# A Mamba block with a routed MLP on one core: the first norm's root and the scaling of duT move to GpSimd instructions of another form

## What is computed

```python
h = _layernorm(x) * (1 + ca) + sa
x = x + ga * _L0_attn_ref(h, ...)      # gate, conv of 4 taps, sigmoid, selective scan over 16 states, product Wo
h = _layernorm(x) * (1 + cb) + sb
x = x + gb * _L0_ffn_ref(h, ...)       # router, 8 experts of 352, top 2
```

## Time and profile before

| | |
|---|---|
| three runs | 697.56, 698.61, 700.04 us |
| the profiled execution | 697.62 us, span 695.80 us |
| busy, share of the span | PE 88%, DVE 79%, ACT 77%, POOL 74%, weight loads 74% |
| mean granted TensorE clock | 0.984 |
| head, to the first scan | 58.2 us |
| steps, first to last scan | 58 to about 513 us |
| the experts' tiles and the combination | to 695.8 us |

### The profile page before, as it was taken

One profiled execution on the slowest core, in us unless ns is written; L12 is line 12 of the kernel. 1 busy time (PEld: TensorE's weight loads), 2 busy tenths in 40 slices (PEclk: granted clock), 3 DMA queues, 4 the chain that ended last, 5 costly groups with the idle time before them and its releaser, 6 DMA issues.

```text
span 695.8 us, 14462 instructions
## 1 busy us (share of the span) xinstructions
PE 615.6 (88%) x4435; PEld 512.3 (74%) x4435; DVE 552.0 (79%) x1170; ACT 535.4 (77%) x1000; POOL 517.3 (74%) x453
## 2 busy tenths in 40 slices
PE   3986889989988998997999898769789999999995
PEld 3444757867767675785777677658578999999994
DVE  4347779999989999999999999989986586555554
ACT  3268998997998997999799799797834756566650
POOL 3147969988799899989989999986964647644441
PEclk9999999999999999999999999899999999999998
DMA  7030336434943454534455335466711223222545
GB/s 237 0 123 2 102 86 161 135 93 129 320 122 106 115 129 128 162 101 109 119 148 136 105 100 129 128 182 178 177 30 55 65 62 86 81 69 65 152 145 193
DMA packets 65194, 82.92 MB, mean 119 GB/s; under 512 B 6960, under 2 KB 55152, under 8 KB 61024
## 3 DMA queue, kind: packets, MB, share of 16 engines
q1 hardware_dynamic: 59648, 70.78, 37.2%
q0 software_dynamic: 4320, 9.12, 4.0%
q10 hardware_dynamic: 1152, 2.10, 0.8%
HBM read 52.19 MB, written 29.78 MB: 118 GB/s over the span
## 4 chain that ended last, share of the span: by engine, by line
PE 43%; ACT 36%; DVE 11%; issue 7%; DMA 1%; POOL 1%; DVEq 0%; SPq 0%; ACTq 0%; POOLq 0%
PE psum L589 26%; PE psum L593 16%; ACT S L1006 12%; ACT dA L1014 11%; DVE ring L1370 5%; ACT L953 1%; ACT xn L918 1%; ACT soft L946 1%; ACT soft L945 1%; ACT soft L953 1%; ACT soft L950 1%; ACT L1014 1%; DMA ring<-results 1%; ACT hT L900 1%; ACT psum L958 1%
## 5 line engine op out<-in xcount | busy, mean ns | idle before, releaser
L559 POOL TENSOR_TENSOR ring<-ring,Cb 128x1024 f32<-128x1024 f32 x128 | 279.6, 2186 | 36.7 <-DVE ring L1370 36.2
L593 PEld LDWEIGHTS psum<-ident,S 128*128 128x128 f32 x1024 | 118.6, 143 | 113.5 <-issue 67.7
L593 PE MATMUL psum<-ident,S 128*128 128x128 f32 x1024 | 159.2, 279 | 42.7 <-DVE ring L1370 14.3
L1014 ACT ACTIVATE dA<-delta,A 128x512 f32<-128x512 f32 x256 | 178.6, 716 | 10.3 <-DVE ring L1370 10.1
L1006 ACT ACTIVATE S<-duT,BT 128x256 f32<-128x256 f32 x384 | 166.4, 501 | 24.3 <-DVE duT L1110 20.2
L593 PE MATMUL psum<-ident,ring 128*128 128x128 f32 x1088 | 159.5, 278 | 4.2 <-DMA ring<-results 3.8
L1370 DVE TENSOR_TENSOR_SCAN ring<-dA,state,psum 128x512 f32<-128x512 f32 x128 | 157.6, 1265 | 1.0 <-PE psum L593 0.4
L1370 DVE TENSOR_TENSOR_SCAN ring<-dA,psum 128x512 f32<-128x512 f32 x128 | 150.2, 1206 | 8.8 <-PE psum L593 8.2
L593 PEld LDWEIGHTS psum<-ident,ring 128*128 128x128 f32 x1088 | 129.5, 144 | 5.2 <-DMA ring<-results 4.3
L581 POOL DMA_INDIRECT results<-xn,result_at x71 | 68.7, 968 | 74.6 <-DVE xn L1503 64.9
L589 PE MATMUL psum<-uT,S 128*128 128x128 f32 x852 | 107.2, 275 | 1.0 <-DVE uT L1481 1.0
(11 more groups left out here) (218 smaller groups left out, 734.2 us busy)
## 6 DMA issues: line engine op xcount, KB each, us to landing
Cb<-c_rows SPq DMA_DIRECT2D x32, 1024.0 KB, 6.0
token_rows<-zeros SPq DMA_DIRECT2D x64, 272.0 KB, 7.1
uT<-token_rows SPq DMA_DIRECT2D x71, 68.0 KB, 1.8
ring<-results SPq DMA_DIRECT2D x8, 512.0 KB, 5.0
xT<-in_xT SPq DMA_DIRECT2D x4, 512.0 KB, 4.9
out_T<-xT ACTq DMA_DIRECT2D x8, 256.0 KB, 2.8
stage<-in_xT SPq DMA_DIRECT2D x6, 256.0 KB, 7.7
gateup_w<-in_gate SPq DMA_DIRECT2D x1, 1408.0 KB, 9.5
```

Source lines behind the costliest of these rows:

```text
L559: nc.gpsimd.tensor_tensor(ring[:, k % RING, :, 0:BANK], ring[:, k % RING, :, 1:], Cb[:, group_ % 2, own, :].unsqueeze(1).to_broadcast([P, ...
L593: return nc.tensor.matmul(out, block_in, ident[at, at], is_transpose=True, start=start, stop=True, skip_group_check=True)
L1014: nc.scalar.activation(dA[:, (k * HALVES + a) % DA_SLOTS, :], delta[:, s % 2, a, :], ACT.Exp, scale=A[:, a, n:n + 1]).then_inc(da_ready, 1)
```

## The change

It has four parts.

1. The root of segments 0 and 1 is taken in the same way as that of the others: DVE adds eps, POOL takes the power, DVE multiplies. ACT's Ln and Exp and four of DVE's five instructions go. The new steps stand right behind the statistics of segment 1, in `front_roots(0, FIRST)`.
2. The root of segments 2 to 7 is shared in the same way: DVE adds eps and later multiplies by minus mean in one instruction, POOL takes the power alone. DVE's two instructions stand right behind its last statistics, in `front_roots(FIRST, CHUNKS)`; POOL's stays in gap 19.
3. For the second norm DVE adds eps, in gap 18.
4. POOL's `scale_in` issues one tensor_scalar for each chunk, with the column of BT as a scalar of each partition and a second operation (times 1.0), in place of one tensor_tensor with a broadcast column. `add_bias` gets a second operation as well (times 1.0, where there was none).

```diff
 def pool_scaled(k):
-    return sum(pool_chunks(j) > 0 for j in range(k + 1))
+    return sum(pool_chunks(j) for j in range(k + 1))
...
-            def root(v, shifted, out, steps, count, done):
-
-                nc.gpsimd.tensor_scalar(shifted, v, LN_EPS, 1.0, ALU.add, ALU.mult).then_inc(steps, 1)
-                pool.wait_ge(steps, count)
-                nc.gpsimd.tensor_tensor(out, shifted, minus_half[:, 0:shifted.shape[1]], ALU.pow).then_inc(done, 1)
+            def front_root(first, last, shifts):
+
+                pool.wait_ge(fshift_ready, shifts)
+                nc.gpsimd.tensor_tensor(frs[:, 0, first:last], frs[:, 0, first:last], minus_half[:, first:last], ALU.pow
+                                        ).then_inc(froot_ready, 1)
...
             def tail_root(f):
-                pool.wait_ge(tstat_ready, CS * (f + 1))
-                root(tstat[:, :, 1], trs[:, 0, :], trs[:, 1, :], tstep, f + 1, trs_ready)
+                pool.wait_ge(tshift_ready, f + 1)
+                nc.gpsimd.tensor_tensor(trs[:, :], trs[:, :], minus_half[:, 0:CS], ALU.pow).then_inc(trs_ready, 1)
...
             def add_bias(b):
                 pool.wait_ge(stat_filled, SEG * (b + 1))
-                nc.gpsimd.tensor_scalar(xT[:, b * SEQ:(b + 1) * SEQ], xT[:, b * SEQ:(b + 1) * SEQ], gabo[:, b:b + 1], None,
-                                        ALU.add).then_inc(gabo_added, 1)
+                nc.gpsimd.tensor_scalar(xT[:, b * SEQ:(b + 1) * SEQ], xT[:, b * SEQ:(b + 1) * SEQ], gabo[:, b:b + 1], 1.0,
+                                        ALU.add, ALU.mult).then_inc(gabo_added, 1)
...
                 if window == -1 and gap == 19:
-                    pool.wait_ge(fstat_ready, CHUNKS)
...
+                    front_root(FIRST, CHUNKS, 2)
...
-                    nc.gpsimd.tensor_tensor(S[:, k % S_SLOTS, CS - own:, :], duT[:, s % 2, CS - own:, :],
-                                            BT[:, s % 2, CS - own:, n:n + 1].to_broadcast([P, own, MLP]), ALU.mult
-                                            ).then_inc(scaled_pool, 1)
-
+                    for c in range(CS - own, CS):
+                        nc.gpsimd.tensor_scalar(S[:, k % S_SLOTS, c, :], duT[:, s % 2, c, :], BT[:, s % 2, c, n:n + 1], 1.0,
+                                                ALU.mult, ALU.mult).then_inc(scaled_pool, 1)
+
+            front_root(0, FIRST, 1)
             pool.wait_ge(mod_step, MOD_STEPS)
...
+                if gap == 18:
+                    dve.wait_ge(tstat_ready, CS * (f + 1))
+                    V.tensor_scalar(trs[:, :], tstat[:, :, 1], LN_EPS, None, ALU.add).then_inc(tshift_ready, 1)
...
+            def front_roots(first, last):
+
+                part = slice(first, last)
+                dve.wait_ge(fstat_ready, last)
+                V.tensor_scalar(frs[:, 0, part], fstat[:, part, 1], LN_EPS, None, ALU.add).then_inc(fshift_ready, 1)
+                dve.wait_ge(froot_ready, int(first > 0) + 1)
+                V.scalar_tensor_tensor(frs[:, 1, part], fstat[:, part, 0], -1.0, frs[:, 0, part], ALU.mult, ALU.mult
+                                       ).then_inc(frs_ready, 1)
+
             for f in range(SEG):
                 raw_stats(f)
+            front_roots(0, FIRST)
...
                     if (window, gap) == (-1, 10):
                         for f in range(SEG + 3, SEGS):
                             raw_stats(f)
+                        front_roots(FIRST, CHUNKS)
```

More of the change, by code:

```diff
@@ L93, in adaln_kernel @@
         xT = sb("xT", [P, NTOK])
+        minus_half = sb("minus_half", [P, NTOK // P])
         ident = sb("ident", [P, P])
@@ L99, in adaln_kernel @@
         zeros = sb("zeros", [P, ROW])
-        eps = sb("eps", [P, 1])
-        minus_half = sb("minus_half", [P, NTOK // P])
         w1c = sb("w1c", [P, CONVK, MLP])
@@ L145, in adaln_kernel @@
         fstat = sb("fstat", [P, CHUNKS, 2])
-        frs = sb("frs", [P, 5, CHUNKS])
+        frs = sb("frs", [P, 2, CHUNKS])
         tbn = sb("tbn", [P, CS, 6])
         tstat = sb("tstat", [P, CS, 2])
-        trs = sb("trs", [P, 2, CS])
+        trs = sb("trs", [P, CS])
         u = sb("u", [P, 2, HALVES, BANK])
@@ L262, in adaln_kernel @@
                              "dbias_filled"))
-        flog, fseed, tstep, trs_ready = (sem(n) for n in ("flog", "fseed", "tstep", "trs_ready"))
-        fstep, frs_ready = ([sem(f"{n}{k}") for k in range(2)] for n in ("fstep", "frs_ready"))
+        trs_ready, froot_ready, frs_ready, fshift_ready, tshift_ready = (
+            sem(n) for n in ("trs_ready", "froot_ready", "frs_ready", "fshift_ready", "tshift_ready"))
         staged = [sem(f"staged{k}") for k in range(2)]
@@ L292, in adaln_kernel @@
         GROUP_STEPS = tuple(steps[-1] for steps in TABLE_STEPS)
-        MOD_STEPS = 26
+        MOD_STEPS = 25
         CONSTS = 9
@@ L912, in front @@
                         act.wait_ge(filled["raw"], f - SEG + 1)
-                    act.wait_ge(frs_ready[int(f >= SEG)], 1)
+                    act.wait_ge(frs_ready, min(f // SEG, 1) + 1)
                     wait(act, filled["xn"], f)
@@ L918, in front @@
                         nc.scalar.activation(xn[0][:, c * P:(c + 1) * P], source[:, c * P:(c + 1) * P], ACT.Identity,
-                                             scale=frs[:, 3, at], bias=frs[:, 4, at]).then_inc(read["raw"], 1)
+                                             scale=frs[:, 0, at], bias=frs[:, 1, at]).then_inc(read["raw"], 1)
                 if gap in (22, 28):
@@ L969, in tail @@
                                    ).then_inc(read["rows"], 1)
[L971 to L979, removed]
             def routing(gap, f):
@@ L1018, in _ @@
             nc.scalar.activation(siluc[:, :], cT[:, :], ACT.Silu).then_inc(siluc_ready, 1)
-            act.wait_ge(mod_step, 2)
-            for step in range(2):
-                front_seeds(step)
             act.wait_ge(loaded["attn"], 16 * ATTN_LOADS)
@@ L1373, in _ @@
             V.memset(mean_w[:, :], 1.0 / HID).then_inc(mod_step, 1)
-            V.memset(eps[:, :], LN_EPS).then_inc(mod_step, 1)
             V.memset(both[:, :], 0.0).then_inc(mod_step, 1)
@@ L1388, in _ @@
             V.tensor_copy(mod[:, :, :], bank(4)[:, 0:6 * BATCH].rearrange("p (k b) -> p k b", k=6)).then_inc(mod_step, 1)
-            dve.wait_ge(mod_step, 14)
+            dve.wait_ge(mod_step, 13)
             gates = mod[:, 2:6:3, :]
             V.tensor_scalar(modt[:, :, :], gates, -1.0, 0.25, ALU.mult, ALU.max).then_inc(mod_step, 1)
-            dve.wait_ge(mod_step, 15)
+            dve.wait_ge(mod_step, 14)
             V.tensor_tensor(modt[:, :, :], modt[:, :, :], gates, ALU.max).then_inc(mod_step, 1)
             V.tensor_scalar(mod[:, 1:5:3, :], mod[:, 1:5:3, :], 1.0, None, ALU.add).then_inc(mod_step, 1)
+            dve.wait_ge(mod_step, 16)
+            V.tensor_scalar(gates, gates, 0.0, 2.0, ALU.is_ge, ALU.mult).then_inc(mod_step, 1)
             dve.wait_ge(mod_step, 17)
-            V.tensor_scalar(gates, gates, 0.0, 2.0, ALU.is_ge, ALU.mult).then_inc(mod_step, 1)
+            V.scalar_tensor_tensor(gates, gates, -1.0, modt[:, :, :], ALU.add, ALU.mult).then_inc(mod_step, 1)
             dve.wait_ge(mod_step, 18)
-            V.scalar_tensor_tensor(gates, gates, -1.0, modt[:, :, :], ALU.add, ALU.mult).then_inc(mod_step, 1)
-            dve.wait_ge(mod_step, 19)
             V.tensor_scalar(gabo[:, :], mod[:, 2, :], bo[:, 0:1], None, ALU.mult).then_inc(mod_step, 1)
@@ L1425, in _ @@
             V.reduce_sum(zhalf[:, :], conv[:, :, :], AX.X).then_inc(const_ready, 1)
[L1427 to L1438, removed]
             V.tensor_tensor(w1c[:, :, :], w1.unsqueeze(1).to_broadcast([P, CONVK, MLP]),
```

7 lines of the change are left out of this document (1 added, 6 removed).

## The result

The change is slower: 707.48 us median of four runs (706.66 to 708.59) against 698.51 of four runs of the kernel before, ratio 1.0132, 95% interval 1.0112 to 1.0151, or 9.0 us. The profiled execution has a span of 704.9 us. The forecast was 701.7, with a range from 694.5 to 706.5: the direction was right, the size was not, and the measured time lies outside the range. Differences between experiments are therefore good to 1 or 2 us, and the ratios to the kernel before are the safer numbers.

What follows compares the result with a forecast made beforehand. The prediction took the chain over PE and ACT as the bound, with POOL busy 74% but 1% of the chain; -0.8 + 4.4 + 0.8 - 1.0 - 0.3 = +3.1 us gave 701.7, range 694.5 to 706.5.

Steps and rivals of the forecast that it cites:

- Small things: Second norm's eps goes from POOL to DVE's idle time at gap 18; with a memset and constants' placement, -0.3 us.
- rival of the prediction: PE's waits for S fully recovered, 697.5 (0.20); POOL pacing the steps, 694.7 (0.17); slower POOL additions and S, 714 (0.13).
- signs of being wrong: POOL's S above 0.6 us; first scan before 61; segments shorter by over 1 us each; first root's power over 2 us.
- the one on segments 2 to 5: Sign of being right in the steps: segments 2 to 5 each shorter by under 0.5 us.
- First root: Head, segments 0 and 1: DVE and POOL replace ACT's root; xn's transposes start at 16.7, not 17.50, -0.8 us.
- Second root: Head, segments 2 to 7: DVE waits for POOL's power of 24 columns ahead of softplus, +4.4 us.
- the clock: Head: PE's clock drops while it waits over 5 us for delta, slowing two groups of transposes, +0.8 us.
- POOL's S: Steps: each 256-column piece takes 0.40 us in the new form, so PE waits less, -1.0 us over the steps.
- the slow form's case: POOL's scaling and bias addition cost 2.58 ns a column after all: +16 us, 714, chance 0.13.
- POOL would now be done well before: Segment 4: POOL's S would end well before PE needs it, but DVE limits the gain to about 0.4 us.
- the four waits of PE: One wait for POOL's S in each of segments 2 to 5; recovered whole, they would bring 4 x 1.3 = 5.2 us.
- Sum: Whole kernel: -0.8 + 4.4 + 0.8 - 1.0 - 0.3 = +3.1 us, 701.7 against the median.

Runs made afterwards that it cites:

- part 3 alone: Kernel before, with only the eps addition for the second norm moved from POOL to DVE in gap 18: 706.95 us, ratio 1.0125.
- part 4 alone: Kernel before, with only POOL's scaling by a scalar of each partition and its two-operation bias addition: 698.08 us of ten runs, ratio 1.0005.

## Why the prediction was wrong, step by step

The step that failed is the one on the second norm's eps, under "Small things"; the others were right, or wrong by 1 us. No rival of the prediction has it, and none of its signs of being wrong would have shown it. Of the signs of being right, the one on segments 2 to 5 failed: they are 3.7 us longer in all, where they were to be shorter.

- **First root.** The term was -0.8: the constants' count at 14.4 (14.35 measured), the power 1.67 (1.68), the taps 18.8 (18.96). Right by its steps, with two details that it did not have: w1c was held up by POOL's addition of the bias, and xbias behind it released the taps. By the time of the last statistics the profiled execution was 2.4 us ahead, not 0.8. The larger part of the difference is the first eight taps, 5.12 us where they took 6.39, both at a recorded clock of 1.00; among the kernels here they take 5.1 to 6.5, and why is open. The other part is that PE then ran at 2.4 GHz where the execution before was at half clock from 42 to 45: the kernel with part 3 alone shows that half clock in the same place, the one with part 4 alone does not, and their softplus starts at 47.27 and 46.07. So the extra 1.6 us of that execution are no merit of the change. Over many runs the first root is worth about 1 us, within the noise.
- **Second root.** The term was +4.4 for the wait and +0.8 for the clock, 5.2 together. Moving the multiplication took back 5.6 (5.1 by the ratios, 4.6 at the first scan). The wait was 4.3 us idle plus two small instructions, and softplus came 4.4 us later behind the statistics than before; the clock fell as said. Right. But the price of a slow group, 1.10 us, was read at 17.50, where the profile gives a granted clock of 1.00 and not 0.50; that the group took 1.11 us at 0.50 was shown only by this run.
- **POOL's S.** Its price was to be 0.40 us and was 0.48, the bias 1.01 and was 1.14: the form with two operations was the right one to follow, and the slow form's case fell. The term was -1.0; measured by part 4 alone it is nothing that can be told from no change, and -0.5 in segments 2 to 5 of the profiled execution. The sentence "POOL would now be done well before" was wrong: it counted POOL's instructions as if they stood back to back, while its waits for scans grew from 36.2 us to 45.7. Its S came half a us earlier, and the four waits of PE gave back 0.4 us in all.
- **Small things.** Here the forecast failed. The passage was: "The second norm's eps goes from POOL (0.19 and a wait of 0.08) to DVE, which has idle time at gap 18", with -0.3 us. The idle time was there (0.3 to 0.9 us before softplus in segments 2 to 5 of the kernel before), but the instruction's price was +5.6 us, by taking it off DVE: it lasted 1.8 to 2.5 us in segments 2 to 6, each time until POOL's ring product ended. I gave DVE's instruction the 0.16 to 0.18 us of small instructions in the head, where POOL was idle or writing constants, and did not ask what POOL does at gap 18 of a step. The rows that I used had no such form of DVE's beside a ring product.
- **Sum.** With the measured terms: -1 + 5.6 + 0 + 5.6 = 10.2, against 9.0 measured in all; each term is good to 1 or 2 us.

## What to carry to other kernels

An instruction added to an engine is priced by its form and by what runs beside it, and not by its size: here 128x4 took 0.16 us in one stage and up to 2.5 in another. If the same small operation ends 0.02 to 0.04 us after an instruction of another engine each time, it was held up inside. Here four instructions of one column, or leaving it on the other engine, freed it. Compare the least and the most of a group of equal shape to find such instructions. And a wait that is moved onto an engine is to be put behind that engine's last urgent work: the same multiplication cost over 5 us ahead of softplus and nothing behind duT.

## What was new about the hardware

- DVE's fp32 tensor_scalar of 128x4 from SBUF to SBUF waited inside itself for POOL's running products to end and lasted 0.94 to 2.8 us, all twelve times in two kernels; four of 128x1 in the same place took 0.31 us together. Of DVE's instructions with two inputs, two of 128x8 beside POOL's addition of the bias took 0.17 us as ever, while w1c, 128x1024, took 2.8 in place of 2.0.
- POOL's tensor_scalar takes 1.14 us for 1024 columns with two operations and 2.87 with one; with a scalar of each partition and two operations, 0.48 for 256 columns, where the product with a broadcast column took 0.62. For the 1024 columns the added second operation, times 1.0, is the only difference.
- POOL's power costs 1.04, 1.68 and 4.2 us for 4, 8 and 24 columns, 0.16 for each further column.
- The granted clock fell to half in PE's idle time of 6.53 us, before the next instruction came at 55.27, and stayed there to 62. Behind an idle time of 2.61 us (the multiplication moved) it fell as well, after the first group of transposes.
